# Second experts' token rows: scattered to their slots ahead of time, with number and weight, instead of gathered from a list

## The chip, the cores and the metric

The kernel runs on one core of one Trainium2 chip. The metric is the device time of one execution in microseconds. The engines are PE (TensorE), ACT (ScalarE), DVE (VectorE), POOL (GpSimd) and SP (SyncE, which here only issues DMAs).

## What is computed

64 batches of 128 tokens of width 128 pass four layers, each added to its input: a cross attention, a mixture of 8 experts with one chosen per token, a block of two attentions with feed-forward parts, and a mixture of 64 experts with four chosen per token and room for 128 tokens each. The change concerns the last:

```python
x = hidden_states.reshape(-1, h)
probs_all = softmax(x @ router_w); top_p, top_i = top_k(probs_all, 4)
...
buf = zeros((64, 128, h)).at[expert_id, pos].set(x[token_idx])   # a slot per token and expert
h1 = einsum('ech,ehf->ecf', buf, w1)
g = silu(h1[..., :64]) * h1[..., 64:]
y = einsum('eci,eih->ech', g, w2)
out = zeros((T, h)).at[token_idx].add(y[expert_id, pos] * prob)
```

Here `x` is the normalised row of the token. A token has four slots, one in the room of each of its experts.

## The kernel before

Five stages follow each other. Each engine has its own instruction stream, written out batch by batch, and semaphores (`s_...`) tie them.

1. First attention with the router of the first experts (`pipeline_a`, 64 batches, several in flight). SP issues loads and the clearing of `c_d` in this stage; its stream names batches but waits for none of them, so it runs ahead as far as its queue lets it.
2. First experts, 72 tiles of 128 tokens (`tile0`). POOL scatters the results into `y0_d`.
3. The two attentions of the block (`pipeline_b`, 128 halves: an even one for the first attention of a batch, an odd one for the second). In its steps `t3` to `t8` the odd halves also carry the router of the second experts: DVE normalises the row into `xnS` (L1368, called in `half_b`), SP stores it to `xn1_d` (`store_xn`, L471), PE, ACT and DVE choose four experts, and DVE writes for each token and choice the slot (`dest`, L1679), the token's number and its weight (`pay`, L1680 and L1681). POOL scatters these pairs of 8 bytes to the slot's place in `list1_d` (`scatter_pick`, L1258), four scatters per batch: choices 1 and 2, then 3, then 0 of the following batch, among the other work of a half.
4. Second experts, 64 tiles, one expert each (`tile1`). SP loads the list (L542). DVE works out the tokens' numbers from it (L1758). POOL gathers 128 rows per tile out of `xn1_d` into a ring of eight buffers `xg` (`gather`, L1198), five tiles ahead of the scatter of the finished rows into `c_d` (`scatter`, L1206). PE transposes a tile (L730), multiplies by the expert's first matrix (L946), transposes the gated half (L922), multiplies by the second matrix (L937); every second tile it also transposes a piece of `pover` (L928). ACT does the silu (L1118) and copies the last slot's row (L1122), which SP stores (`store_last`, L548). DVE does the gate (L1765), the result times the weight (L1786) and the copies of the transposes (L1359).
5. Final sum: SP loads four rows per token from `c_d` (L566), POOL and DVE add them, SP stores `out`.

In the trace DRAM tensors and SBUF tiles stand by their names without numbers: `xn_d` is `xn1_d`, `list_d` is `list0_d` or `list1_d`, `xs_d` is `xs_d`. Where tiles share memory the trace has the memory's name: `xg` is `qT`, `yS` is `vS`, the list is `kbd`, `xgT`, `silu` and `glu` are `pTm`, `h0T` is `pT`, `hT` is `shared`, `ylast` is `oT`.

In the second attention ACT's half ends so (`half_b`):

```python
af(vS[0:h.T, h.slot, :], dbank[0:h.T, :], ACT.Copy).then_inc(s_v, 1)
if t5 and t5.a:
    act.wait_ge(s_v8, t5.b(1, 1))
    af(expl[:, :], lg[:, :], ACT.Exp, bias=nv0[:, :], accum_out=esum[:, :])
    af(e4[:, :], v8[:, 0:TOPK], ACT.Exp, bias=nv0[:, :]).then_inc(s_el, 1)
if t2:
    act.wait_ge(s_li2, t2.l(1, 1))
    ... four Gelu activations into hT, s_gelu
```

Of the kernel before, what the change touches and what calls it, by code (L numbers as in the profile page):

```python
# [4 lines left out]
F32 = mybir.dt.float32  # L5
# [41 lines left out]
def build_program(nc, t, out, NB=64):  # L47
# [12 lines left out]
    xn1_d = nc.dram_tensor("xn1_d", (NTOK, P), F32).ap()  # L60
    list1_d = nc.dram_tensor("list1_d", (SLOTS1, 2), F32).ap()
# [4 lines left out]
    with ctx:  # L66
# [19 lines left out]
        cst = sb("cst", [P, CST_WIDTH])  # L86
# [8 lines left out]
        pick = cst[:, 318:830].rearrange("p (c t) -> p c t", c=4)  # L95
        dimcol = cst[:, 830:958].rearrange("p (g m) -> p g m", g=NG)
        kone = cst[:, 958:962]
        qmask = cst[:, 962:964]
# [23 lines left out]
        kT = sb("kT", [P, 512])  # L122
# [60 lines left out]
        pay = sb("pay", [P, 2, TOPK, 2])  # L183
        pay_i = pay[:, :, :, :].bitcast(I32)
# [35 lines left out]
        list1 = kbd[:, 0, 0:2 * E1].rearrange("p (e c) -> p e c", c=2)  # L220
        list1_i = list1.bitcast(I32)
        ids1 = kbd[:, 2, 0:E1].bitcast(I32)
# [69 lines left out]
        s_xnd = [sem("s_xnd_even"), sem("s_xnd_odd")]  # L292
# [6 lines left out]
        s_idx = sem("s_idx")  # L299
# [7 lines left out]
        s_l1 = sem("s_l1")  # L307
# [12 lines left out]
        NINIT = -(-(SLOTS0 // P) // P) + 1  # L320
# [91 lines left out]
        def _(sp):  # L412
            x_v = t["x"].rearrange("b s d -> s b d")
            c_v = t["ctx"].rearrange("b s d -> s b d")
            sp.dma_start(cst[:, :], t["cst"]).then_inc(s_const, 16)
# [25 lines left out]
            def start_lists():  # L441

                sp.wait_ge(s_const, 48)
# [6 lines left out]
                list1_v = list1_d.rearrange("(p e) c -> p (e c)", e=E1)  # L450
                sp.dma_start(list1_v, padlist1[:, :].bitcast(F32)).then_inc(s_init, 16)
# [16 lines left out]
            def store_xn(v, dst):  # L468
                sp.wait_ge(s_xn, v.gb(1, 1))
                sp.nop(nofuse=True)  # L470
                sp.dma_start(dst[bass.ds(v.batch * P, P), :], xnS[:, v.bs, :])\  # L471
                    .then_inc(s_xnd[v.bs], 16)

            def half_a(at):
# [45 lines left out]
            def half_b(at):  # L520
# [8 lines left out]
                if t3 and t3.a:  # L529
                    store_xn(t3, xn1_d)  # L530
# [9 lines left out]
            for s in range(2):  # L540
                sp.wait_ge(s_sc1[s], 64 * (NB // 2))
            sp.dma_start(list1[:, 0:E1, :], list1_d.rearrange("(p e) c -> p e c", e=E1))\  # L542
                .then_inc(s_l1, 16)

            def store_last(i, k, more):
# [3 lines left out]
                    .then_inc(s_yld[k], 16)  # L549

# [35 lines left out]
            for s in range(2):  # L586
                sp.wait_ge(s_xnd[s], 16 * (NB // 2))
# [5 lines left out]
        def _(pe):  # L593
# [14 lines left out]
            pe.wait_ge(s_const, 48)  # L608
# [112 lines left out]
            def tokens_in(u, q):  # L721
# [8 lines left out]
                tr(bank[q][:, 0:P], xg[:, k, :], ident).then_inc(s_gt, 1)  # L730
# [255 lines left out]
        def _(act):  # L986
# [79 lines left out]
            def half_b(at):  # L1066
# [76 lines left out]
        def _(pool):  # L1143
# [13 lines left out]
            pool.wait_ge(s_const, 48)  # L1157
# [36 lines left out]
            def gather(u, k, src, at):  # L1194
                if positive(n := u.count(1, 1 - RING)):
                    pool.wait_ge(s_gt, n)
                    pool.nop(nofuse=True)
                g_.indirect_dma_start(out=xg[:, k, :], out_offset=None, in_=src,  # L1198
                                      in_offset=bass.IndirectOffsetOnAxis(ap=at.bitcast(U32), axis=0))\
                    .then_inc(s_g[k], 16)  # L1200

            def scatter(u, k, dst, at):
# [4 lines left out]
                    ap=at.bitcast(U32), axis=0), in_=yS[:, k, :], in_offset=None,  # L1207
# [712 lines left out]
```

## Time and profile before

| | |
|---|---|
| median of 3 runs | 2568.9 us (2567.36 to 2571.63) |
| profiled execution | 2574.55 us, its span 2572.8 us |
| PE busy | 2296.9 us, 89% |
| DVE busy | 1961.4 us, 76% |
| ACT busy | 1605.9 us, 62% |
| POOL busy | 1597.4 us, 62% |
| moved by DMA | 96.04 MB, mean 37 GB/s |
| TensorE's granted clock, mean | 0.919 of 2.4 GHz |

The span runs from the first to the last instruction in the profile. The shares are means over five stages with different limits, so the sections below go by stage.

### The profile page before, as it was taken

To read this page: it belongs to the slowest core of one execution; us is meant where nothing else is said; L and a number is where in the kernel's file an instruction comes from. 1 tells how busy PE (TensorE), PEld (TensorE's weight loads), DVE (VectorE), ACT (ScalarE), POOL (GpSimd) and SP (SyncE) were. 2 spreads that over 40 slices of the span, in tenths; PEclk is the share of its full clock that TensorE was granted. 3 is DMA by queue.
4 is the path that set the end of the run, shared out by engine and by line. 5 is a ranking of instruction groups with operands and counts; after the bars stand their busy time and mean duration, and the time that the engine had idled before them with its cause. 6 is when DMAs were issued, how large, how long until landed. Compare 5 with 4: busy or idle time off the path is not lost. (4 is left out here: it accounts for less than half of the span.)

```text
span 2572.8 us, 87802 instructions
## 1 busy us (share of the span) xinstructions
PE 2296.9 (89%) x31528; PEld 1793.1 (70%) x31528; DVE 1961.4 (76%) x6039; ACT 1605.9 (62%) x3346; POOL 1597.4 (62%) x2574
## 2 busy tenths in 40 slices
PE   6889999958878999999999999999999999866766
PEld 5667777737876777777777777777777777644544
DVE  4678788756665788888888888888888888853448
ACT  4556566524544777778777777777777778741110
POOL 1445555543544577777777776777777777646766
PEclk9989999979988999999999999999999999965555
DMA  9930000012210011100000000000000000001138
GB/s 220 237 68 11 11 11 12 11 27 58 55 36 5 6 41 41 39 9 9 9 8 7 9 9 9 7 9 9 9 6 9 9 9 8 5 5 40 49 103 262
DMA packets 132234, 96.04 MB, mean 37 GB/s; under 512 B 42483, under 2 KB 114765, under 8 KB 131422
## 3 DMA queue, kind: packets, MB, share of 16 engines
q1 hardware_dynamic: 113118, 74.05, 11.0%
q0 software_dynamic: 18688, 16.39, 2.3%
q8 instruction: 256, 4.19, 0.8%
q14 instruction: 172, 1.41, 0.3%
HBM read 51.59 MB, written 40.02 MB: 36 GB/s over the span
## 5 line engine op out<-in xcount | busy, mean ns | idle before, releaser
L1258 POOL DMA_INDIRECT list_d<-pay,dest x256 | 268.6, 1049 | 135.0 <-issue 76.9
L1687 DVE TENSOR_REDUCE rdx<-core 128x16 f32<-128x1920 f32 (+1 forms) x128 | 282.8, 2209 | 38.9 <-PE core L790 38.7
L1148 POOL TENSOR_SCALAR st_h<-st_h 128x1 f32<-128x1 f32 x192 | 44.0, 229 | 356.9 <-DVE st_h L1365 355.0
L1091 ACT ACTIVATE kbd<-core 128x1024 f32<-128x1024 f32 (+1 forms) x256 | 245.7, 1011 | 8.8 <-PE core L828 8.8
L823 PE MATMUL core<-qT,pTm 32*128 32x128 f32 (+1 forms) x4096 | 195.1, 306 | 0.4 <-ACT nm3T L1077 0.4
L790 PEld LDWEIGHTS core<-pTm,qT 32*128 32x128 f32 x4096 | 125.8, 186 | 97.8 <-ACT qT L1095 93.2
L823 PEld LDWEIGHTS core<-qT,pTm 32*128 32x128 f32 (+1 forms) x4096 | 162.3, 186 | 19.4 <-issue 11.0
L1108 ACT ACT_TABLE_LOAD x128 | 164.2, 1283 | 2.3
L776 PE MATMUL bank<-yT,wk 128*128 128x128 f32 (+1 forms) x1024 | 148.9, 288 | 18.4 <-DVE denT L1626 12.4
L1420 DVE TENSOR_REDUCE rdx<-core 128x8 f32<-128x960 f32 x128 | 142.4, 1153 | 27.1 <-PE core L625 26.2
L1086 ACT ACT_TABLE_LOAD x124 | 159.1, 1283 | 2.2
L1080 ACT ACTIVATE pTm<-bank 128x480 f32<-128x480 f32 (+1 forms) x128 | 74.7, 584 | 130.9 <-PE bank L776 130.9
L776 PE MATMUL bank<-zT,wq 128*128 128x128 f32 x1024 | 150.7, 291 | 1.0 <-DVE oT L1708 1.0
L790 PE MATMUL core<-pTm,qT 32*128 32x128 f32 (+1 forms) x4096 | 149.8, 282 | 0.2 <-ACT qT L1095 0.2
L776 PEld LDWEIGHTS bank<-yT,wk 128*128 128x128 f32 (+1 forms) x1024 | 124.9, 191 | 35.8 <-DVE denT L1626 32.5
L861 PE MATMUL bank<-li,shared 128*128 128x128 f32 x1024 | 144.2, 285 | 6.0 <-ACT shared L1108 5.9
L1108 ACT ACTIVATE shared<-bank,b2c 128x128 f32<-128x128 f32 x512 | 145.9, 368 | 2.5 <-PE bank L897 0.9
L897 PE MATMUL bank<-z3T,li 128*128 128x128 f32 x1024 | 140.6, 282 | 0.8 <-ACT z3T L1083 0.6
L798 PE MATMUL bank<-kbd,cst 128*32 128x512 f32 (+1 forms) x1024 | 138.7, 614 | 2.4 <-ACT kbd L1091 2.3
L776 PEld LDWEIGHTS bank<-zT,wq 128*128 128x128 f32 x1024 | 126.4, 194 | 18.8 <-issue 10.0
L1100 ACT ACTIVATE vS<-bank 120x512 f32<-120x512 f32 (+1 forms) x128 | 76.4, 597 | 97.7 <-PE bank L910 97.7
L910 PE MATMUL bank<-wv,yT 128*128 128x512 f32 (+1 forms) x256 | 137.1, 616 | 0.0
(242 smaller groups left out, 7045.5 us busy)
## 6 DMA issues: line engine op xcount, KB each, us to landing
c_d<-zeros SPq DMA_DIRECT2D x64, 256.0 KB
big<-c_d SPq DMA_DIRECT2D x64, 256.0 KB, 3.6
big<-in_w SPq DMA_DIRECT2D x3, 2048.0 KB, 8.6
qT<-xs_d SPq DMA_DIRECT2D x72, 64.0 KB, 1.8
yb<-y_d SPq DMA_DIRECT2D x64, 64.0 KB, 1.9
xn_d<-xnS SPq DMA_DIRECT2D x64, 64.0 KB, 1.5
list_d<-pay,dest POOLq DMA_INDIRECT x256, 2.2
out<-big SPq DMA_DIRECT2D x64, 64.0 KB
```

The source lines that it names most:

```text
L776: last = mm(b[:, c * T:(c + 1) * T], w[:, c * P:(c + 1) * P], x, start=True, stop=True)
L790: last = mm(core[:, g, c * T:(c + 1) * T], qT[r, s, c * P:(c + 1) * P], kT2[r, s, c * T:(c + 1) * T], start=True, stop=True)
L798: last = mm(dbank[32 * g:32 * g + 32, :], ones32[0:t.T, :], pTb[0:t.T, g, :], start=True, stop=True)
L823: mm(core[0:T, g, c * P:(c + 1) * P], kT2[r, s, c * T:(c + 1) * T], qT[r, s, c * P:(c + 1) * P], start=(c == 0), stop=False, skip_group_ch ...
L861: last = mm(m1[:, 0:P], hT[:, c * P:(c + 1) * P], li3[t3.a][:, c * P:(c + 1) * P], start=(c == 0), stop=(c == 3))
L897: last = mm(m1[:, c * P:(c + 1) * P], li2[t2.a][:, c * P:(c + 1) * P], z3T[:, :], start=True, stop=True)
L1086: af(e_warm[:, :], neghalf[:, :], ACT.Exp)
L1091: af(pTb[0:u.T, 2 * k:2 * k + 2, :], core[0:u.T, 2 * k:2 * k + 2, :], ACT.Exp, scale=SCALE).then_inc(s_pexp, 1)
L1108: last = af(hT[:, c * P:(c + 1) * P], m1[:, c * P:(c + 1) * P], ACT.Gelu, bias=b2c[t2.a][:, c:c + 1])
L1258: g_.indirect_dma_start(out=list1_d, out_offset=bass.IndirectOffsetOnAxis(ap=dest[:, v.bs, k:k + 1], axis=0), in_=pay[:, v.bs, k, :], in_o ...
L1420: last = v_.tensor_reduce(nma[:, 16:P + 16].rearrange("p (g k) -> p g k", g=NG)[:, 2 * k:2 * k + 2, 0:4], core[:, 2 * k:2 * k + 2, 0:4 * C ...
L1687: v_.tensor_reduce(nm_part[0], core[:, :, 0:4 * T].rearrange("p g (c t) -> p g c t", c=4), AX.X, ALU.max, negate=True)
```

## The change

Each batch's normalised row goes straight to its four slots in DRAM, together with the token's number and weight. A new tensor `xs1_d` has 8,192 slots of 130 words: 128 of the row, the number, the weight. It takes the place of `xn1_d` and `list1_d`. SP clears it in the first attention at batch 18 (the rows with zeros, the two last words with the padding that the list had). In the second attention ACT copies the normalised row four times into `xpay`, beside the number and weight that DVE writes there, and POOL's four scatters per batch carry 520 bytes a row instead of 8. In the second experts SP loads a tile's slots with one plain DMA into a ring of eight (`xg1`, in the memory of `vS`), tile j + 8 after scatter j has landed; number and weight come with the row, so the list, the numbers' computation and the 64 gathers are gone. The results move to the memory of `qT`. To make room the constants are loaded in three DMAs, one of them (`pick`) into `rS`.

```diff
-    xn1_d = nc.dram_tensor("xn1_d", (NTOK, P), F32).ap()
-    list1_d = nc.dram_tensor("list1_d", (SLOTS1, 2), F32).ap()
+    xs1_d = nc.dram_tensor("xs1_d", (SLOTS1, P + 2), F32).ap()
...
-        pay = sb("pay", [P, 2, TOPK, 2])
-        pay_i = pay[:, :, :, :].bitcast(I32)
+        xpay = sb("xpay", [P, 2, TOPK, P + 2])
+        pay = xpay[:, :, :, P:P + 2]
+        pay_i = xpay[:, :, :, :].bitcast(I32)[:, :, :, P:P + 2]
...
+        xg1 = v_all[:, 0:RING * (P + 2)].rearrange("p (b d) -> p b d", d=P + 2)
+        xg1_i = xg1.bitcast(I32)
+        yS1 = xg
...
-            sp.dma_start(cst[:, :], t["cst"]).then_inc(s_const, 16)
+            sp.dma_start(cst[:, 0:318], t["cst"][:, 0:318]).then_inc(s_const, 16)
+            sp.dma_start(cst[:, 318:452], t["cst"][:, 830:964]).then_inc(s_const, 16)
+            sp.dma_start(rS[:, :], t["cst"][:, 318:830]).then_inc(s_const, 16)
...
-                sp.dma_start(list1_v, padlist1[:, :].bitcast(F32)).then_inc(s_init, 16)
+            def start_rows1():
+                sp.dma_start(xs1_v[:, :, 0:P], zeros[:, :].unsqueeze(1).to_broadcast([P, E1, P]))\
+                    .then_inc(s_init1, 16)
+                sp.dma_start(xs1_v[:, :, P:P + 2],
+                             padlist1[:, :].bitcast(F32).rearrange("p (e c) -> p e c", c=2)).then_inc(s_init1, 16)
...
+                if u and u.batch == 18:
+                    start_rows1()
...
-                if t3 and t3.a:
-                    store_xn(t3, xn1_d)
...
-            sp.dma_start(list1[:, 0:E1, :], list1_d.rearrange("(p e) c -> p e c", e=E1))\
-                .then_inc(s_l1, 16)
+            def load_rows1(j):
+                if positive(n := j // RING):
+                    sp.wait_ge(s_ysc[j % RING], 16 * (TILES0 // RING + n))
+                    sp.nop(nofuse=True)
+                sp.dma_start(xg1[:, j % RING, :], xs1_v[:, j, :]).then_inc(s_g[j % RING], 16)
+            for j in range(RING):
+                load_rows1(j)
...
             def store_last(i, k, more):
...
+                if i * RING + k + RING < E1:
+                    load_rows1(i * RING + k + RING)
...
                 if t5 and t5.a:
+                    act.wait_ge(s_xn, t5.gb(1, 1))
+                    if positive(n := t5.pair(64)):
+                        act.wait_ge(s_sc1[t5.bs], n)
+                    af(xpay[:, t5.bs, :, 0:P], xnS[:, t5.bs, :].unsqueeze(1).to_broadcast([P, TOPK, P]), ACT.Copy)\
+                        .then_inc(s_xpay, 1)
...
+            pool.wait_ge(s_c0, 16 * (CROWS // (4 * P)))
+            pool.wait_ge(s_init1, 32)
...
+                    pool.wait_ge(s_xpay, v.b(1, 1))
                     pool.wait_ge(s_dest, v.gb(1, 1))
                     pool.nop(nofuse=True)
-                    g_.indirect_dma_start(out=list1_d, out_offset=bass.IndirectOffsetOnAxis(
-                        ap=dest[:, v.bs, k:k + 1], axis=0), in_=pay[:, v.bs, k, :],
+                    g_.indirect_dma_start(out=xs1_d, out_offset=bass.IndirectOffsetOnAxis(
+                        ap=dest[:, v.bs, k:k + 1], axis=0), in_=xpay[:, v.bs, k, :],
...
-            experts(E1, TILES0, 5, xn1_d, c_d, lambda j: ids1[:, j:j + 1],
-                    lambda j: list1_i[:, j, 0:1], indices_there)
+            for j in range(E1):
+                scatter(Unit(TILES0, 0, RING, j), j % RING, c_d, xg1_i[:, j % RING, P:P + 1], yS1)
...
-                    if positive(n := t3.pair(16)):
-                        dve.wait_ge(s_xnd[t3.bs], n)
+                    if positive(n := t3.b(1, -1)):
+                        dve.wait_ge(s_xpay, n)
...
-            dve.wait_ge(s_l1, 16)
-            v_.tensor_scalar(ids1, list1_i[:, :, 0], 2, NTOK - 1, ALU.logical_shift_right,
-                             ALU.bitwise_and).then_inc(s_idx, 1)
...
-                v_.tensor_scalar(yS[:, k, :], bank[6 + k % 2][:, 0:P], list1[:, j, 1:2], None,
+                v_.tensor_scalar(yS1[:, k, :], bank[6 + k % 2][:, 0:P], xg1[:, k, P + 1:P + 2], None,
                                  ALU.mult).then_inc(s_y, 1)
```

On ACT, in a half of the second attention that carries a router's exponents, the order before is (`vS` are the values, `expl` and `e` the exponents, `shared` Gelu's result, the table load is for Gelu):

```order
L1095 ACTIVATE qT<-bank 128x512 [waits s_qps]
L1100 ACTIVATE vS<-bank 120x512 [waits s_val,s_vps]
L1103 ACTIVATE expl,esum<-lg,nv 128x64 [waits s_v8]
L1104 ACTIVATE e<-v,nv 128x4
L1108 ACT_TABLE_LOAD
L1108 ACTIVATE shared<-bank,b2c 128x128 [waits s_li2]
```

With the change it is:

```order
L1102 ACTIVATE qT<-bank 128x512 [waits s_qps]
L1107 ACTIVATE vS<-bank 120x512 [waits s_val,s_vps]
L1112 ACTIVATE xpay<-xnS 128x4x128 [waits s_sc1_even,s_xn]
L1115 ACTIVATE expl,esum<-lg,nv 128x64 [waits s_v8]
L1116 ACTIVATE e<-v,nv 128x4
L1120 ACT_TABLE_LOAD
L1120 ACTIVATE shared<-bank,b2c 128x128 [waits s_li2]
```

One activation of 512 elements per partition stands ahead of the exponents and Gelu, once per batch.

On POOL, at the end of the second attention and the start of the second experts, the order before is:

```order
L1258 DMA list_d<-pay,dest 8192x2 [waits s_dest] x9
L1198 DMA qT<-xn_d,kbd 128x128 [waits s_idx,s_c0,s_xnd_even,s_xnd_odd,s_gt]
L1198 DMA qT<-xn_d,kbd 128x128 [waits s_gt] x5
L1206 DMA c_d<-vS,kbd 32768x128 [waits s_y]
L1198 DMA qT<-xn_d,kbd 128x128 [waits s_gt]
L1206 DMA c_d<-vS,kbd 32768x128 [waits s_y]
```

With the change POOL has there, and SP has (its first rows are the loads of tokens and of the first eight tiles):

```order
L1258 DMA xs_d<-xpay,dest 8192x130 [waits s_xpay,s_dest] x9
L1210 DMA c_d<-qT,vS 32768x128 [waits s_y] x64
...
L529 DMA yb<-y_d 128x128 [waits s_x2] x49
L547 DMA vS<-xs_d 128x130 [waits s_sc1_odd,s_sc1_even]
L547 DMA vS<-xs_d 128x130 x7
L555 DMA y_d<-oT 1x128 [waits s_yl]
L547 DMA vS<-xs_d 128x130 [waits s_ysc0]
L555 DMA y_d<-oT 1x128 [waits s_yl]
L547 DMA vS<-xs_d 128x130 [waits s_ysc1]
```

The gathers between POOL's scatters are gone, and between two of SP's stores of a last row (`oT`) now stands a load that waits for the scatter eight tiles back.

## Rows read from the trace of the kernel before

**Rows 1.** Page, part 2: the span in 40 slices
```profile
PEclk9989999979988999999999999999999999965555
DMA  9930000012210011100000000000000000001138
```
**Rows 2.** Busy time by stretch: us; PE, PEld, DVE, ACT, POOL (count); PEclk, DMA share, GB/s
```profile
1000.00:1500.00 500.00, 488.05 (x7251) 382.53 (x7254) 437.16 (x1230) 395.08 (x777) 356.48 (x625) 1.00 0.06 17
...
2320.00:2490.00 170.00, 126.31 (x416) 85.15 (x416) 75.49 (x291) 31.24 (x127) 124.50 (x127) 0.50 0.16 46
```
**Rows 3.** Timeline, second experts, POOL: start us, us, engine, line, [idle before]
```profile
2475.44 1.01 POOL L1206 DMA_INDIRECT c_d<-vS,kbd  x1 [0.30 <-issue]
2476.76 0.97 POOL L1198 DMA_INDIRECT qT<-xn_d,kbd  x1 [0.30 <-issue]
2478.03 1.01 POOL L1206 DMA_INDIRECT c_d<-vS,kbd  x1 [0.30 <-issue]
```
**Rows 4.** Timeline, second experts, PE weight loads of the first product
```profile
2330.95 0.50 PEld L946 LDWEIGHTS core<-big,pTm 128*128 128x128 f32 x2 [0.79 <-DVE pTm L1359]
...
2339.76 0.50 PEld L946 LDWEIGHTS core<-big,pTm 128*128 128x128 f32 x2 [0.78 <-DVE pTm L1359]
...
2485.39 0.50 PEld L946 LDWEIGHTS core<-big,pTm 128*128 128x128 f32 x2 [0.68 <-DVE pTm L1359]
```
**Rows 5.** Timeline, second experts, one tile's loop
```profile
2331.78 0.22 ACT L1118 ACTIVATE pTm<-core 128x64 f32<-128x64 f32 x1 [1.60 <-PE core L946]
...
2332.31 0.35 DVE L1786 TENSOR_SCALAR vS<-bank,kbd 128x128 f32<-128x128 f32 x1
...
2332.78 0.28 DVE L1359 COPY pTm<-core 128x128 f32<-128x128 f32 x1
...
2333.11 0.80 PE L946 MATMUL core<-big,pTm 128*128 128x128 f32 x2 [0.51 <-DVE pTm L1359]
...
2333.51 1.01 POOL L1206 DMA_INDIRECT c_d<-vS,kbd  x1 [2.28 <-DVE vS L1786]
```
**Rows 6.** Chain of waits between second attention and second experts: start us, us, what
```profile
2318.87 2.10 DMA list_d<-pay,dest
...
2321.03 1.74 DMA kbd<-list_d
...
2323.96 2.52 DMA qT<-xn_d,kbd
...
2326.73 0.46 PE core L730
```
**Rows 7.** DMA issues: out<-in, count, KB each, us to landing
```profile
qT<-xs_d SPq DMA_DIRECT2D x72, 64.0 KB, 1.8
```
**Rows 8.** ACT's copies of 512 elements from SBUF: ns min/median/max, first and last start
```profile
  L1038 ACT ACTIVATE kbd<-big x72: 629/631/637, 570.0 to 742.7; 128x512 f32 x72
```
**Rows 9.** Timeline, second attention, a half with the router's exponents
```profile
1605.10 0.60 ACT L1100 ACTIVATE vS<-bank 120x512 f32<-120x512 f32 x1 [0.92 <-PE bank L910]
...
1605.59 0.34 ACT L1103 ACTIVATE expl<-lg,nv 128x64 f32<-128x64 f32 x1
...
1607.52 1.14 ACT L1108 ACTIVATE shared<-bank,b2c 128x128 f32<-128x128 f32 x4
...
1608.82 1.06 PE L861 MATMUL bank<-li,shared 128*128 128x128 f32 x8
...
1610.43 0.97 PEld L776 LDWEIGHTS bank<-yT,wk 128*128 128x128 f32 x8 [0.23 <-DVE denT L1626]
```
**Rows 10.** First attention: a busy-time stretch, a wait (74 to 88 us), a timeline row
```profile
75.00:150.00 75.00, 61.80 (x994) 46.34 (x992) 47.04 (x180) 37.35 (x92) 34.83 (x56) 0.89 1.06 232
...
PE core L625 <- issue: 3.0, 1, 3.0
...
145.40 1.50 PE L659 MATMUL bank<-kbd,vS 120*32 120x128 f32 x21 [4.62 <-issue]
```
**Rows 11.** Timeline, start, SP's issue of a constant
```profile
1.25 0.41 SPq L416 DMA_DIRECT2D cst_i<-in_cst_i  x1
```

More of the change, by code:

```diff
@@ L94, in build_program @@
         tilenum = cst[0:1, 238:238 + TILES0]
[L95 to L98, printed above, removed]
+        dimcol = cst[:, 318:446].rearrange("p (g m) -> p g m", g=NG)
+        kone = cst[:, 446:450]
+        qmask = cst[:, 450:452]
         padlist0 = cst_i[:, 0:128]
@@ L306, in build_program @@
         s_w1 = sem("s_w1")
-        s_l1 = sem("s_l1")
+        s_xpay = sem("s_xpay")
+        s_init1 = sem("s_init1")
         s_sil = sem("s_sil")
@@ L466, in _ @@
             n_c = CROWS // (4 * P)
[L468 to L472, printed above, removed]
             def half_a(at):
@@ L585, in _ @@
             sp.wait_ge(s_c0, 16 * n_c)
-            for s in range(2):
-                sp.wait_ge(s_xnd[s], 16 * (NB // 2))
         @block.tensor
@@ L1191, in _, with scatter @@
             pipeline_a(pool, half_a)
[L1194 to L1202, printed above, removed]
+            def scatter(u, k, dst, at, src):
                 pool.wait_ge(s_y, u.count(1, 1))
@@ L1219, in context_roots @@
                     .then_inc(s_crstd, 1)
-            def experts(n, base, lag, src, dst, from_rows, to_rows, ready):
-                for j in range(n + lag):
-                    if j < n:
-                        ready(j)
-                        gather(Unit(base, 0, RING, j), j % RING, src, from_rows(j))
-                    if j >= lag:
-                        scatter(Unit(base, 0, RING, j - lag), (j - lag) % RING, dst, to_rows(j - lag))
             def ids_there(j):
@@ L1237, in _ @@
                 ids_there(j)
-                scatter(Unit(0, 0, RING, j), j % RING, y0_d, tile_rows(j))
+                scatter(Unit(0, 0, RING, j), j % RING, y0_d, tile_rows(j), yS)
+            pool.wait_ge(s_c0, 16 * (CROWS // (4 * P)))
+            pool.wait_ge(s_init1, 32)
             def mask_pair(u, k):
@@ L1319, in _ @@
             pipeline_b(pool, half_b)
-            for s in range(2):
-                pool.wait_ge(s_xnd[s], 16 * (NB // 2))
-            pool.wait_ge(s_c0, 16 * (CROWS // (4 * P)))
-            def indices_there(j):
-                if j == 0:
-                    pool.wait_ge(s_idx, 1)
-                    pool.nop(nofuse=True)
-            experts(E1, TILES0, 5, xn1_d, c_d, lambda j: ids1[:, j:j + 1],
-                    lambda j: list1_i[:, j, 0:1], indices_there)
+            for j in range(E1):
+                scatter(Unit(TILES0, 0, RING, j), j % RING, c_d, xg1_i[:, j % RING, P:P + 1], yS1)
             def step_c(i, k):
@@ L1375, in _ @@
             v_.memset(v_all[:, :], 0.0).then_inc(s_made, 1)
-            dve.wait_ge(s_const, 48)
+            dve.wait_ge(s_const, 80)
             copy(count0[:, :], slot0)
-            copy(pickb[:, :, :], pick)
+            copy(pickb[:, :, :], rS[:, :].rearrange("p (c t) -> p c t", c=4))
             copy(identb[:, :], ident)
```

23 lines of the change are left out of this document (8 added, 15 removed).

## The prediction

> **What bounds the kernel now.** I read the page first, for the slices and the clock, then the busy time by stage, then the timeline of two stages, and the chain of waits only at the seam between them. The program has five stages in time: the first attention, the first experts, the second attention, the second experts (the last stage but one, from about 2,320 us) and the final sum. The page shows TensorE granted 9 tenths of its clock nearly everywhere and 5 tenths in the last four slices, and the DMA engines full only at the start and the end [rows 1].
>
> In the second attention PE is busy 97.6% of a 500 us stretch and POOL 71% [rows 2], so PE's own order sets the pace there. In the second experts it is the other way round. Over 170 us PE is busy 74% at a clock of 0.50 (1.2 GHz) and POOL 73% [rows 2], but the timeline shows that POOL's share is its limit: each tile costs a gather of 0.97 us and a scatter of 1.01 us, each followed by 0.30 us of issue, and they follow each other without another wait. From one scatter to the next it is 2478.03 - 2475.44 = 2.59 us [rows 3]. There is a stretch in which the gathers had run ahead and POOL was not yet the limit. There the first product of a tile starts at 2330.95 and, four tiles later, at 2339.76, which is 2.20 us a tile [rows 4]. That pace is made by a loop through three engines: product (0.80 us at 1.2 GHz) from 2333.11, silu on ACT (in the tile before: 2331.78), then DVE's gate, result (2332.31) and transpose copy, the copy of the next tile's transpose (2332.78), next product [rows 5].
>
> **Term 1: the gathers leave POOL, -20.2 us.** 64 gathers go; 64 scatters stay. POOL then needs 1.01 + 0.30 = 1.31 us a tile [rows 3], less than the 2.20 of the loop, so the loop becomes the bound. The third tile's product starts at 2330.95 and the last (64th) tile's at 2485.39: 61 steps in 154.4 us. 61 steps of 2.20 are 134.2 us, 20.2 less. PE and DVE do the same work as before, and the clock is left at 1.2 GHz. The lower end is 0 (the loads take the gathers' place as limit, a rival below), the upper end a loop at the higher clock (another rival).
>
> What takes the gathers' place is SP's work. Per tile SP waits for tile j's last row, stores it, waits for scatter j, and loads tile j + 8. The nearest load is the one from xs_d in the first experts: 64 KB, 1.8 us to landing [rows 7]. Scatter j's data are ready 5.6 us after its tile entered (first transpose 2326.73, first result 2332.31 [rows 5, 6]); I add 0.85 us to reach POOL (2332.31 + 0.35 to 2333.51 [rows 5]), 2.5 us to landing as a gather takes (2323.96 to its end, [rows 6]), some 0.4 us on SP (the issue of [rows 11]) and 1.8 us for the load: 11.2 us, against 8 x 2.20 = 17.6 us that the ring of eight allows. So the waits on SP cost nothing as long as the round stays under 17.6 us; the store queued behind them is read only at the end.
>
> **Term 2: the seam, -3.5 us.** Now the last scatter of the list starts at 2318.87 and takes 2.10 us, the list is read in 1.74 us from 2321.03, DVE shifts it, POOL starts the first gather at 2323.96, which lands after 2.52 us, and PE starts at 2326.73 [rows 6]. Afterwards a load of 1.8 us starts where the list's did: PE at about 2322.9, 3.8 us earlier. I give back 0.3 because 520 bytes a row land later than 8; POOL's own time for a scatter hardly depends on the row (0.98 for list rows of 8 bytes, 1.01 for rows of 512 bytes [rows 3, 6]). DVE's clearing of glu loses its wait and moves ahead, under cover.
>
> **Term 3: a copy on ACT in the second attention, +8 us.** Once per batch ACT makes four copies of the normalised rows, 512 elements wide, placed behind the copy of the values and ahead of the router's exponents. The same shape from SBUF takes 631 ns [rows 8]; the value copy of 0.60 us and the next activation start 0.49 us apart [rows 9], so I take 0.52 us. Behind it, in the same half, stands the Gelu whose result PE's product L861 waits for. Gelu now ends at 1607.52 + 1.14 = 1608.66 and L861 starts at 1608.82 [rows 9]: of that 0.16 us some 0.05 is the hand-over, 0.1 is slack. If L861 slips, the next place where PE waits anyway is L776, where its weight load sits idle 0.23 us for the transposed denominators, until 1610.43 [rows 9]. 0.52 - 0.1 - 0.23 = 0.19 us gets through, less up to 0.1 that the starts between L861 and L776 still hold. I take 0.13 x 62 batches = 8 us. Beyond that nothing absorbs it, since PE is the bound. The ends are 0 and 0.52 x 64 = 33 us. The waits in front of the copy are for rows normalised two halves before and scatters issued one half before: free. The four scatters per batch stay on POOL at the same price, and the 64 stores that SP made of the rows go, off the path.
>
> **Term 4: more DMA in the first attention, +4 us.** At batch 18 SP issues the clearing of 8,192 rows (4.2 MB) and of their 8-byte ends, between the clearing of c_d and the experts' weights. SP isn't paced by the batches; its queue keeps the DMA engines full until about 150 us (share 1.06 and 232 GB/s between 75 and 150 us [rows 10]; the page's slices are 9, 9, 3, then 0 [rows 1]). 4.2 MB at 232 GB/s is 18 us more of that, and up to as much again for the small rows. Two things could suffer. The first experts' weights are first read at 570.0 us [rows 8]: nothing. PE, however, stood still for 4.62 us in the middle of a run of equal products at 140.8 us with nothing to wait for in the data [rows 10]; I read that as instructions arriving late through full DMA engines, and there is one more such stop, of 3.0 us, between 74 and 88 us [rows 10]. One more is 4.6 us; I take 4, between 0 and 14 (two more, each with its time to refill the pipeline).
>
> The Trainium skill (Runtime: NRT & Kernel Launch, Instruction fetch mechanics) says that crossing an instruction block is "mostly hidden" for straight code. By that rule this term would be 0 and the sum 4 us better; the trace's 4.62 us stand against it.
>
> **Term 5: the start, +0.9 us.** The constants come in three DMAs instead of one. SP spends 0.41 us and a little more on each [rows 11], and the first batch waits for the last weight behind them. The row for the list's padding, 64 KB, leaves the start, off the path.
>
> **Sum.** -20.2 - 3.5 + 8 + 4 + 0.9 = -10.8 us. The profiled execution took 2574.55 us with a span of 2572.8; this gives 2563.8 for it. The median of the three runs is 2568.9, 5.65 us under the profiled one, so I forecast **2558 us**. About 0.2% (5 us) is what a measurement of this kernel can tell from no change: faster means under 2563.8, slower over 2574.0.
>
> **Rivals.**
> (a) *The copy on ACT is paid in full.* If the slack at L861 and L776 is taken up by ACT's other waits, 33 instead of 8 us: 2568.9 + 14.2 = 2583, slower. It decides from 0.13 + 10.8/62 = 0.30 us a batch on. For it: PE 97.6% busy, so every slip counts. Against it: the idle 0.23 at L776 stands in the rows.
> (b) *The clock rises in the second experts.* PE would be busier per us. Halving the product's 0.80 us takes 0.4 us out of the loop: 61 x 0.4 = 24 us as a bound, I take 20: 2538. Against it: in the stretch at 2.20 us a tile the clock stayed at 1.2 GHz, as it did for all 170 us [rows 1, 2]. The Trainium skill (TensorE: Matmul & The Clock Gate, Part 1) calls the throttled state the default that activity releases; by that rule a denser PE could get there.
> (c) *Full DMA engines cost more.* Two or three more stops in the first attention, +14 instead of +4: 2568, no change. For it: two in the present 75 us of overlap; against: whole batches between them ran undisturbed under the same load.
> (d) *The loads replace the gathers as the limit.* If the round of scatter and load through SP takes 20.7 us instead of 11.2, tiles stay at 2.59 us: 2568.9 + 9.4 = 2578, slower; the change then doesn't do what it says. Above 17.6 us it begins to cost. For it: SP waits in order, 128 rows spaced 33 KB apart in DRAM; against: 6 us of room.
>
> **Chances.** Forecast 0.55, (a) 0.10, (b) 0.12, (c) 0.13, (d) 0.10. The forecast's own range is 2548 to 2568 (term 3 from 0 to 16, term 4 from 0 to 10): it gives 0.43 faster, 0.11 the same, 0.01 slower. (b) is faster; (c) is 0.03 faster, 0.08 the same, 0.02 slower; (a) and (d) are slower but for 0.01. Faster 0.58, same 0.20, slower 0.22. For 8 in 10 the range takes in (c), most of (d) and the near part of (b): 2541 to 2579.
>
> **What would show it.** Tiles of the second experts 2.20 us apart, with POOL idle in between waiting for DVE, and SP's loads landing long before PE takes them; the first transpose some 3.5 us after the last scatter landed; halves of the second attention with the copy longer by 0.1 to 0.2 us and the others unchanged; one more stop of PE between 150 and 180 us. The prediction is wrong if the halves grow by over 0.3 us a batch, if PE waits on the loads tile by tile, or if the clock goes to 2.4 GHz after 2,320 us.

## The result, and the profile after

The changed kernel takes 2556.36 us (median of 20 runs), the one before 2569.57 us (20 runs beside it): ratio 0.9957, 95% interval 0.9941 to 0.9973, by that ratio some 11 us faster. The profiled execution of the changed kernel took 2559.96 us, with a span of 2558.1; the one before 2574.55 and 2572.8. Single runs spread over 19 us before and 32 us after, so the stages of the profiles tell more than whole times of one run.

By stages, first to last of the same instruction in both profiles:

| stretch | before | after | difference |
|---|---|---|---|
| first attention, 63 batches | 514.8 | 522.4 | +7.7 |
| from there to the second attention | | | -2.2 |
| second attention, 127 halves | 1511.9 | 1525.9 | +13.9 |
| seam to the first expert product | 38.1 | 34.4 | -3.7 |
| second experts, first to last product | 158.2 | 124.3 | -33.9 |
| after it, final sum | 87.1 | 90.6 | +3.5 |

The page's slices of the changed kernel, which answer to [rows 1]:

```profile
PEclk9889999978997999999999999999999999985775
DMA  9990000002210011100000000000000000000247
```

A third slice is full of transfers, and the last four have a clock of 5, 7, 7, 5 (in tenths of full speed) where all four had 5. The busy time by stretch (columns as in [rows 2]) shows the new shape of the second experts and the fuller start [rows 2, 10]:

```profile
75.00:150.00 75.00, 63.89 (x939) 48.39 (x943) 45.03 (x167) 34.20 (x86) 31.86 (x51) 0.82 1.21 164
160.00:210.00 50.00, 48.46 (x814) 37.54 (x814) 39.50 (x141) 29.79 (x77) 26.29 (x42) 0.94 0.70 165
...
2355.00:2475.00 120.00, 79.53 (x382) 60.55 (x381) 61.83 (x266) 29.48 (x119) 59.29 (x61) 0.73 0.23 61
```

POOL falls from 73% to 49% of the second experts, and the granted clock rises from 0.50 to 0.73. The timeline of POOL in the low-clock part, where [rows 3] had gather and scatter in turn, 0.30 us apart:

```profile
2362.46 0.97 POOL L1210 DMA_INDIRECT c_d<-qT,vS  x1 [1.27 <-DVE qT L1773]
2364.62 0.97 POOL L1210 DMA_INDIRECT c_d<-qT,vS  x1 [1.19 <-DVE qT L1773]
```

Scatters are 2.16 and 2.24 us apart in turn, and POOL waits 1.2 us for DVE before each. PE's weight loads for the first product of a tile, which answer to [rows 4], first at 1.2 GHz, then at 2.4:

```profile
2357.68 0.50 PEld L953 LDWEIGHTS core<-big,pTm 128*128 128x128 f32 x2 [0.91 <-DVE pTm L1351]
2359.93 0.50 PEld L953 LDWEIGHTS core<-big,pTm 128*128 128x128 f32 x2 [0.79 <-DVE pTm L1351]
...
2455.20 0.30 PEld L953 LDWEIGHTS core<-big,pTm 128*128 128x128 f32 x2 [0.91 <-DVE pTm L1351]
2456.91 0.30 PEld L953 LDWEIGHTS core<-big,pTm 128*128 128x128 f32 x2 [1.02 <-DVE pTm L1351]
```

The same loop takes 2.20 us at 1.2 GHz and 1.71 at 2.4. Of the 63 steps 31 were slow (mean 2.21), 29 at the faster pace or near it, and one between. The first two take 1.57 and 1.82 us in the kernel before as well and were still at 1.2 GHz.

At the seam the chain of waits, against [rows 6], has lost the list and the gather:

```profile
2338.29 2.12 DMA xs_d<-xpay,dest
...
2340.47 1.77 DMA vS<-xs_d
2342.24 0.25 issue
2342.49 0.46 PE core L737
```

From the start of the last scatter's transfer to the first transpose it is 4.20 us; in [rows 6] it was 2326.73 - 2318.87 = 7.86.

In the second attention, ScalarE's timeline of a half with the router's exponents, which answers to [rows 9]:

```profile
1618.07 0.60 ACT L1107 ACTIVATE vS<-bank 120x512 f32<-120x512 f32 x1 [0.92 <-PE bank L917]
1618.56 0.63 ACT L1112 ACTIVATE xpay<-xnS 128x512 f32<-128x512 f32 x1
1619.08 0.34 ACT L1115 ACTIVATE expl<-lg,nv 128x64 f32<-128x64 f32 x1
...
1621.01 1.14 ACT L1120 ACTIVATE shared<-bank,b2c 128x128 f32<-128x128 f32 x4
```

The exponents start 0.52 us later behind the new copy, and so does the Gelu. In the page's part 5 of the changed kernel (busy us, mean ns | idle before and its releaser), the product that reads the Gelu's result now waits:

```profile
L868 PE MATMUL bank<-li,shared 128*128 128x128 f32 x1024 | 147.5, 288 | 31.6 <-ACT shared L1120 31.5
```

Before, the same group (L861 there) waited 6.0 us, 5.9 of them for the Gelu.

Behind the last computation stands one more difference. At the end of the program every engine has a drain instruction. GpSimd's is the last to end with the change (2549.1 + 8.8 = 2557.9 of 2558.1 us); before, it had ended at 2571.8, ahead of SyncE's at 2572.6 (min/median/max ns, start us; `L66` before, `L65` after):

```profile
L66 POOLq DRAIN  x1: 3403/3403/3403, 2568.4 to 2568.4; - x1
```
```profile
L65 POOLq DRAIN  x1: 8803/8803/8803, 2549.1 to 2549.1; - x1
```

### The profile page after: what moved, and what is told of

It reads as the page before. It is cut to its first block and busy times, and to the rows that moved or that the text cites. A ratio compares the mean times of both kernels' runs of the same rounds, so it can differ in the third digit from the quotient of the medians.

```text
span 2558.1 us, 87791 instructions
## 1 busy us (share of the span) xinstructions
PE 2261.2 (88%) x31528; PEld 1777.5 (69%) x31528; DVE 1955.0 (76%) x6038; ACT 1635.4 (64%) x3410; POOL 1539.6 (60%) x2510
## 5 line engine op out<-in xcount | busy, mean ns | idle before, releaser
L1258 POOL DMA_INDIRECT xs_d<-xpay,dest x256 | 267.8, 1046 | 138.1 <-issue 133.5
L783 PE MATMUL bank<-yT,wk 128*128 128x128 f32 (+1 forms) x1024 | 147.8, 287 | 19.5 <-DVE denT L1618 17.5
L868 PEld LDWEIGHTS bank<-li,shared 128*128 128x128 f32 x1024 | 125.8, 193 | 47.3 <-ACT shared L1120 43.0
L783 PE MATMUL bank<-zT,wq 128*128 128x128 f32 x1024 | 150.3, 291 | 1.0 <-DVE oT L1700 1.0
L783 PEld LDWEIGHTS bank<-yT,wk 128*128 128x128 f32 (+1 forms) x1024 | 126.3, 193 | 30.2 <-DVE denT L1618 27.0
L783 PEld LDWEIGHTS bank<-zT,wq 128*128 128x128 f32 x1024 | 126.3, 194 | 18.7 <-issue 9.9
```

Of the source, the lines that this page charges most:

```text
L783: last = mm(b[:, c * T:(c + 1) * T], w[:, c * P:(c + 1) * P], x, start=True, stop=True)
L868: last = mm(m1[:, 0:P], hT[:, c * P:(c + 1) * P], li3[t3.a][:, c * P:(c + 1) * P], start=(c == 0), stop=(c == 3))
L1258: g_.indirect_dma_start(out=xs1_d, out_offset=bass.IndirectOffsetOnAxis(ap=dest[:, v.bs, k:k + 1], axis=0), in_=xpay[:, v.bs, k, :], in_of ...
```

## The experiments

Ratios are to the kernel before, run beside each. "Pair" is the mean of 56 pairs of halves in the middle of the second attention (before 23.23 us, after 23.47), "stage" the second experts as in the table. Columns of the profile lines are those of the views above.

### The copy on ScalarE

**early_copy.** The copy moves ahead of the wait for the values:

```diff
+                if t5 and t5.a:
+                    act.wait_ge(s_xn, t5.gb(1, 1))
+                    ...
+                    af(xpay[:, t5.bs, :, 0:P], xnS[:, t5.bs, :]...., ACT.Copy).then_inc(s_xpay, 1)
                 if h:
                     act.wait_ge(s_vps, h.l(1, 1))
```

> ScalarE's copy of the normalised rows into the payload is issued ahead of its copy of vS instead of behind it; nothing else changes. Theory (the copy delays the router's Exp and with it the Gelu, and by that each pair of halves of the second attention): the mean pair falls from the changed kernel's 23.47 us back to about 23.25, and the whole by 8 to 13 us against the changed kernel, to about 2,545. Rival 1 (the pair grew because the four scatters now carry 520 bytes a row, or for another reason than ScalarE's order): the pair stays at 23.4 to 23.5 and the whole within 3 us. Rival 2 (vS becomes the late one): the pair grows to 23.7 or more.

Measured: 2542.54 us, ratio 0.9907 (0.9884 to 0.9930), pair 23.28. The copy fills time in which ScalarE waited for PE anyway, 0.92 us before and 0.40 now:

```profile
1609.88 0.64 ACT L1107 ACTIVATE xpay<-xnS 128x512 f32<-128x512 f32 x1
1610.93 0.60 ACT L1113 ACTIVATE vS<-bank 120x512 f32<-120x512 f32 x1 [0.40 <-PE bank L917]
1611.42 0.34 ACT L1116 ACTIVATE expl<-lg,nv 128x64 f32<-128x64 f32 x1
```

and the product's wait for the Gelu on the page is back to where it was:

```profile
L868 PE MATMUL bank<-li,shared 128*128 128x128 f32 x1024 | 144.7, 285 | 6.1 <-ACT shared L1121 5.6
```

The theory held, rivals 1 and 2 fell: the copy's place costs 0.19 us a pair, 11 us over the 56 pairs of that stretch. The whole fell by 13.8 us against the changed kernel, a little more than the 8 to 13 expected.

**short_copy.** One column of each row is copied instead of 128, so the second experts work on wrong rows:

```diff
-   af(xpay[:, t5.bs, :, 0:P], xnS[:, t5.bs, :].unsqueeze(1).to_broadcast([P, TOPK, P]), ACT.Copy)
+   af(xpay[:, t5.bs, :, 0:1], xnS[:, t5.bs, 0:1].unsqueeze(1).to_broadcast([P, TOPK, 1]), ACT.Copy)
```

> The copy on ScalarE moves one column of each of the four payload rows instead of 128 (the payload is zero otherwise), so that the second experts work on wrong rows; the instruction, its waits and the four scatters of 520 bytes a row stay. Theory (the copy's length is what the pair lost): the copy takes 0.2 to 0.25 us instead of 0.63, and the mean pair comes to 23.27 to 23.35 us. Rival (the scatters' bytes or the instruction's waits are what costs): the pair stays at 23.4 to 23.5.

Measured: 2534.85 us, ratio 0.9876 (0.9849 to 0.9904), the copy 0.20 us, pair 23.20, a little below what was expected. So it is the copy's length behind which the Gelu stood, and the 520-byte scatters cost the pair nothing that shows.

### GpSimd in the second experts

**gather_back.** An unread gather behind each scatter, which waits for the last one:

```diff
                 scatter(Unit(TILES0, 0, RING, j), ...)
+                if j + 1 < E1:
+                    if j:
+                        pool.wait_ge(s_dum, 16 * j)
+                    g_.indirect_dma_start(out=kbd[:, 0, 0:P], in_=y0_d, in_offset=... ids[:, 0:1] ...).then_inc(s_dum, 16)
```

> Behind each scatter of the second experts GpSimd issues one indirect gather of 128 rows into a tile that nothing reads, as before the change but with no one waiting for the data. Theory (GpSimd with two indirect DMAs of some 1.1 us each set the 2.53 us step before): the step grows from 2.20 (or 1.72 where the clock is at 2.4 GHz) to 2.3 to 2.6 us at either clock, the stage from 124 us to 145 to 165, and the whole by 20 to 40 us. Rival (the step fell because loads by SP arrive earlier, or because the list and its waits are gone): with loads untouched here, the step stays at 1.72 to 2.20 and the whole within 5 us.

Measured: 2635.85 us, ratio 1.0270 (1.0242 to 1.0298), stage 193 us, steps of 3.1. That is more than the theory said, and the timeline tells why: GpSimd waited 0.9 us for its own gather to land, which the kernel before did not do:

```profile
2441.03 1.03 POOL L1329 DMA_INDIRECT kbd<-y_d,denT  x1 [0.89 <-DMA kbd<-y_d,denT]
```

The edit had added a wait besides the work, so it was made again without it.

**gather_ring.** The same with four targets and four semaphores; GpSimd waits for the gather of four steps ago.

> As the run with the gathers back, but the unread gathers go to a ring of four tiles with a semaphore each, so that GpSimd waits for the gather of four steps ago and not for the last. The first run waited for its own last gather each step. Theory (GpSimd's issuing of two indirect DMAs is the limit of the step before the change): steps of 2.3 to 2.6 us, stage 150 to 160, whole 25 to 35 us over the changed kernel. Rival (the wait alone made the 3.25 us of that run): steps of 2.20 or 1.72, whole within 5 us of the changed kernel.

Measured: 2592.3 us, ratio 1.0097 (1.0078 to 1.0117), stage 157.2 us, 61 steps of 2.52 in the mean where the kernel before had 2.53. POOL's timeline is that of [rows 3] again:

```profile
2441.22 1.01 POOL L1211 DMA_INDIRECT c_d<-qT,vS  x1 [0.30 <-issue]
2442.54 1.03 POOL L1329 DMA_INDIRECT kbd<-y_d,denT  x1 [0.31 <-issue]
2443.87 1.01 POOL L1211 DMA_INDIRECT c_d<-qT,vS  x1 [0.30 <-issue]
```

Nobody read these gathers, the loads by SyncE were untouched, and the whole gain of the stage was gone. GpSimd's issue of two indirect DMAs a tile was the bound, and the rival fell. The whole is 36 us over the changed kernel, 25 to 35 expected. The granted clock fell back with it, to 0.51 from 2,355 to 2,495 us, where the changed kernel had 0.73.

### The first attention

**before_again.** The kernel before, unchanged.

> The kernel before, unchanged, for a second profile. Theory (its first attention has stops as irregular as the changed kernel's): 510 to 524 us for the first attention against 514.8 in the first profile, pair 23.23 and expert step 2.53 us unchanged. Rival (the changed kernel's additional transfers make it longer by 5 us or more each time): 515 or less here too, where the changed kernel and its variants show 517 to 524.

Measured: 2568.56 us in one run; first attention 510.3 us, pair 23.29, expert steps of 2.56. Six kernels with the changed kernel's first attention (it, early_copy, short_copy, gather_back, gather_ring, early_warm) show 517.2 to 524.0, mean 520.6, against 514.8 and 510.3: 8 us more in the mean, with no overlap. The lengthening is very likely real, though two profiles of before are few. A kernel without the two clears would be the direct test of their cost. It has no measurement here.

**rows_clear_late.** The slots' clears at batch 40 (`u.batch == 18` becomes `u.batch == 40`).

> The changed kernel with the two transfers that clear the slots (4 MB of rows, and the pieces of 8 bytes) issued at batch 40 of the first attention instead of batch 18; as SyncE doesn't wait there, they stand only behind more clears in its queue. Theory (these two make one or two stops wherever they run): the stops move or stay, first attention 517 to 524 us as before, whole within 3 us. Rival (it matters that they join the other traffic at its height): first attention at or under 515, as in the kernel before, and the whole 5 us or more less.

Measured: 2560.51 us, ratio 0.9975 (0.9955 to 0.9994; its interval overlaps the changed kernel's), first attention 520.9 us. No change that can be told, as the theory said: SyncE runs so far ahead of the batches that "batch 40" is only a place in its queue.

**merged_rows.** One transfer of 520-byte rows instead of rows of 512 bytes and ends of 8:

```diff
-   sp.dma_start(xs1_v[:, :, 0:P], zeros...to_broadcast([P, E1, P]))
-   sp.dma_start(xs1_v[:, :, P:P + 2], padlist1...)
+   sp.dma_start(xs1_v[:, :, :], xpay[:, 0, 0:1, :].to_broadcast([P, 64, P + 2]))
```

> The changed kernel with the slots cleared by one transfer of whole rows of 520 bytes (zeros, and number and weight of an empty slot, laid out once in the payload buffer) instead of rows of 512 and pieces of 8 bytes. Theory (the 8,192 pieces of 8 bytes, between batches 9 and 13 or so, make the additional stops of the first attention): first attention falls from 517 to 524 us to 510 to 515, and the DMA share of the stretch from 110 to 210 us falls from 1.16 and 0.70 to about 0.9 and 0.3; whole 5 to 8 us less than the changed kernel. Rival 1 (it is the 4 MB): unchanged within 3 us. Rival 2 (luck): anything between 510 and 524.

Measured: 2545.1 us, ratio 0.9919 (0.9896 to 0.9942), but first attention 519.1 us. The DMA share from 160 to 210 us fell from 0.70 to 0.48, yet the stops stayed (14.0 us in four from 60 to 225 us), so the theory failed: the small pieces alone don't make them. The whole was some 11 us faster all the same, and in the profile nearly all of it lies elsewhere: 50 of the 63 expert steps ran at the faster pace instead of 29, stage 113.5 instead of 124.3. Why this edit should do that isn't known.

**early_paced.** The early copy, and SyncE keeps step with the batches:

```diff
                 if u:
+                    sp.wait_ge(s_q, u.n(1, 1))
                     sp.dma_start(c_rows[u.batch], zeros4).then_inc(s_c0, 16)
```

> The early copy, and besides SyncE waits, before each of the 64 clears of the result rows that it issues in the first attention, until that batch's qT is there; so the clears, and the slots' clears and the weights behind them, come batch by batch. Theory (the stops of TensorE in the first 220 us, 7 to 9 of one to nine us over the undisturbed batch of 7.6, happen because its instructions are fetched behind the full queues): the first attention falls from 517 to 524 us to about 490 to 500, and the whole by 20 to 30 against the early copy alone, to about 2,515 to 2,523. Rival (the stops come at places in the program, whatever the DMA engines do): first attention stays at 515 to 525 and the whole within 5 us of 2,542.

Measured: 2534.65 us, ratio 0.9874 (0.9853 to 0.9895), first attention 509.8 us. The first attention gained half of what was expected (14 us against early_copy), the whole a third (8 us instead of 20 to 30). The windows show where PE still lost time:

```profile
60.00:110.00 50.00, 47.97 (x860) 37.65 (x860) 40.30 (x157) 31.86 (x80) 27.45 (x46) 1.00 0.28 79
110.00:160.00 50.00, 45.93 (x802) 35.04 (x799) 39.13 (x141) 29.30 (x74) 27.34 (x44) 1.00 0.37 79
160.00:210.00 50.00, 42.52 (x673) 32.60 (x667) 31.54 (x117) 24.65 (x64) 21.90 (x35) 0.86 1.26 106
```

With the engines at a share of 0.28 PE ran undisturbed from 60 to 110 us; between 160 and 210, where the slots' clears go out in one piece, the share is 1.26 and PE is busy 5 us less. Most of that is a wait of another kind than the stops marked "issue". PE waited 4.8 us for GpSimd's `big`, and GpSimd had waited 5.5 us for its own scatter to land:

```profile
POOL big L1169 <- DMA xs_d<-big,dest: 5.5, 1, 5.5
PE bank L693 <- POOL big L1169: 4.8, 1, 4.8
```

**spread.** The early copy, the pacing, and the slots cleared by rows of 520 bytes in eight transfers, one at every other batch from 30 to 44.

> The early copy, SyncE's pacing of the clears, and the slots cleared by rows of 520 bytes in eight transfers, at batches 30 to 44. Theory (stops come where the DMA engines are full, and the stops of the paced run at 165 to 220 us are the slots' clears): first attention falls from 509.8 us to 492 to 502, the whole by 8 to 17 us to about 2,520 to 2,527. Rival (stops belong to the weights' loads or to places in the program): first attention 505 to 512, whole within 5 us of 2,535.

Measured: 2508.24 us, ratio 0.9789 (0.9767 to 0.9810), first attention 492.1 us, stage 111.6 us. The whole is lower than expected because 54 of the expert steps happened to run at the faster pace. No batch of the first attention took over 10 us but the first. Waits of PE from 60 to 225 us (engine, line, releaser: us in total, times, longest), of the changed kernel:

```profile
PE bank L666 <- issue: 8.4, 3, 4.5
PE core L632 <- issue: 5.2, 2, 4.0
PE core L644 <- DVE qT L1422: 4.1, 14, 0.3
```

and of this one:

```profile
PE core L647 <- DVE qT L1426: 6.4, 22, 0.3
PE bank L705 <- DVE rdx L1416: 0.6, 2, 0.4
PE bank L669 <- issue: 0.5, 1, 0.5
```

The stops with nothing to wait for in the data, 13.6 us in five, are down to 0.5 in one. The same rows are cleared. So the stops are long where the DMA engines are full.

What is late there is PE's instructions, and the kept traces show it. Part 3 of the page lists a queue of kind "instruction", `q8`, with 256 packets of 16 KB, while PE's stream has 65,705 records: one packet for 256 records. With 160 more records (spread_seam) it has 257 packets. Two facts tie the stops to it. Numbered from the start of the stream, 53 of the 55 stops of 0.9 us or more marked "issue" between 60 and 330 us, over all 14 profiles, stand 193 to 196 records behind a multiple of 256. (The two others stand 71 behind; one of them lasts 2.9 us in early_warm, where the DMA share had been 0.05 for 9 us.) In the changed kernel each of its five stops ends 1.4 to 2.7 us after a packet of this queue has landed. One of them lasts from 98.36 to 102.33 us. Below are lines of the queues from 90 to 99 us, lines of the queues from 99 to 102.3 us, and PE's row (packets, MB, share of 16 engines for the queues):

```profile
q1 hardware_dynamic: 2268, 1.16, 117.0%
q0 software_dynamic: 64, 0.07, 5.1%
```
```profile
q1 hardware_dynamic: 1088, 0.56, 121.3%
q8 instruction: 1, 0.02, 2.9%
```
```profile
102.33 2.10 PE L632 MATMUL core<-pTm,qT 32*128 32x240 f32 x16 [3.97 <-issue]
```

The packet starts at 99.14 us, when PE already stands still. From 160 to 300 us of the same run the packets start 153 to 266 records before PE would reach that place.

A stop costs more than its idle time. The stops marked "issue" sum to 10.3 us in the kernel before, 13.6 in the changed one and 0.5 here, but the granted clock from 60 to 225 us is 0.93, 0.88 and 1.00: behind a long stop PE works for a while at 1.2 GHz. The same 32 products of L644 take 1.92 us at 109.69 us, in the 9 us behind this stop with a clock of 0.50, and 1.15 us at 95.56 us at full speed.

### The clock in the second experts

**early_warm.** The early copy, 40 unread products ahead of the stage, and one in each step:

```diff
+   for j in range(40):
+       mm(bank[1][:, 2 * P:3 * P], ident, ident, start=True, stop=True)
    tokens_in(Unit(TILES0, 0, RING, 0), 0)
    ...
    mm(bank[2 + q][:, 0:P], xgT[:, q, :], ...).then_inc(s_hps, 1)
+   mm(bank[1 - q][:, 2 * P:3 * P], ident, ident, start=True, stop=True)
```

> The early copy, and besides TensorE does one more 128 by 128 product by ident in each step of the second experts, in an unused part of a bank, and 40 of them ahead of the first step; nothing reads them. Theory (TensorE's clock falls because it waits too much there, and its granted clock of 1.2 GHz makes the steps of 2.20 us where 2.4 GHz gives 1.72): more of the steps are at 1.72 us, 50 or more of 63, and the stage takes 110 to 115 us instead of 122 to 124; whole 8 to 14 us under the early copy alone. Rival 1 (the added product lies on TensorE's path at 1.2 GHz): steps of 2.4 to 2.5 us, whole 5 to 15 us more. Rival 2 (the clock doesn't follow this activity): the pattern of steps stays, whole within 3 us.

Measured: 2538.84 us, ratio 0.9896 (0.9878 to 0.9913), not to be told from the early copy alone. The clock did what the theory said (55 of 63 steps at 1.88 and the first two shorter, mean clock 0.94 from 2,316 to 2,416 us), but the product itself adds 0.17 us to each step, so the stage took 119.6 us instead of 122.5: -3, not -8 to -14.

**spread_seam.** The spread version and the 40 products ahead of the stage, none in the steps.

> The spread version, and 40 unread products by ident ahead of the first step of the second experts; none in the steps. Theory (TensorE busy ahead of the stage raises its clock to 2.4 GHz, and the steps alone keep it there for part of the stage): the first steps are 1.72 us instead of 2.20, stage 108 to 112 us, whole 0 to 6 us under the spread version. Rival (without work in each step the clock falls again at once): steps of 2.20 in the first 9 as in the spread version or soon after, whole the same or slower by the products' own time where the first load is already there.

Measured: 2504.06 us, ratio 0.9773 (0.9744 to 0.9802). No step over 1.72 us, stage 107.5. TensorE's timeline shows the 40 products (two passes each) end to end, and the clock has risen by the time the stage begins:

```profile
2290.18 11.80 PE L975 MATMUL core<-cst 128*128 128x128 f32 x80 [0.69 <-DVE count L1660]
2301.82 0.27 PE L740 MATMUL core<-cst,vS 128*128 128x128 f32 x1
2302.47 0.49 PE L956 MATMUL core<-big,pTm 128*128 128x128 f32 x2 [0.38 <-DVE pTm L1357]
```

The first product of the stage takes 0.49 us here; at 1.2 GHz it took 0.80 [rows 5].

On the whole time it can't be told from the spread version. In the profiles its expert stage is 4 us shorter and its first attention 4.6 us longer, with one stop of 2.6 us at 155.2 us. The DMA share was only 0.42 from 140 to 160 us there, so pacing makes such stops rare and doesn't rule them out. It is the fastest median of the study.

**spread_fill32.** As spread_seam, with a product of 32 columns in each step (`ident[:, 0:32]`).

> The spread version, the 40 products ahead of the stage, and in each step an unread product of 32 columns instead of 128. Theory (the product of 128 columns added 0.17 us to the step at 2.4 GHz because it lay on TensorE's path; one of 32 takes less than half of that): steps of 1.76 to 1.80 us throughout, stage 112 to 114 us, equal to the spread version within 4 us but steadier. Rival (32 columns are too few to hold the clock): stretches of 2.25 us steps remain.

Measured: 2558.44 us, ratio 0.9967 (0.9951 to 0.9983). 54 us slower than without the small product. The rival in the extreme: after two steps the clock fell to 1.2 GHz and stayed there. Windows of spread_seam and of this run, 2,316 to 2,416 us:

```profile
2316.00:2416.00 100.00, 55.58 (x366) 41.86 (x364) 55.31 (x254) 28.22 (x114) 57.11 (x59) 1.00 0.27 70
```
```profile
2316.00:2416.00 100.00, 82.92 (x323) 67.70 (x323) 42.24 (x173) 18.77 (x76) 36.88 (x38) 0.50 0.18 47
```

At the low clock the steps are 2.63 us, 0.43 more than without it: the added product of 0.47 us now lies on the path as well. Why the clock fell with this product in each step and stayed up without it isn't known.

## Why the prediction was right, and where it was not

The forecast was 2558 (faster), the result 2556.36. That it is so near is luck. In the profiles the span fell by 14.7 us, forecast 10.8: the clock gave some 14 us that the sum did not have, the copy and the first attention took some 10 more than it had, and the seam came out as forecast. The mechanisms of terms 1 to 3 hold, the nearness of the sum comes from errors that cancel. By the prediction's own sign of being wrong, a clock of 2.4 GHz after 2,320 us, its picture of the last stage failed. One sum is off as well: term 3 from 0 to 16 and term 4 from 0 to 10 make a range of 2546 to 2572, not 2548 to 2568.

**Term 1** (gathers leave POOL, -20.2): right in mechanism and size at the clock it assumed. The slow steps are 2.21 us against the forecast 2.20 and 2.53 before; 61 steps of 2.21 would be 19.6 us less than the 154.4. gather_ring undid it alone and got the old step back. The stage gained 33.9, and the other 14 us are **rival (b)**, the higher clock, in 29 of the 63 steps. I had priced it as all or nothing and given it 0.12; "in the stretch at 2.20 us a tile the clock stayed at 1.2 GHz" was read from the first tiles only, before POOL became the limit. The second profile of before, taken later, has two steps of 1.71 among its first eight, so the faster step occurs there too. A clock that comes in part should have been a term with its own range.

**Term 2** (seam, -3.5): measured -3.66 between the same two events, by the steps forecast.

**Term 3** (copy on ScalarE, +8): mechanism right, size too small: +0.19 to 0.24 us a batch, 11 to 14 us, where I took 0.13. The failing step is the cover taken off at L776, 0.23 us. [rows 9] shows that as idle time of the weight load. PE's own row for the same products has no idle time marked, and starts 0.09 us behind the end of the one before:

```profile
1610.11 0.23 PE L872 MATMUL bank<-identb,rdx 128*128 128x128 bf16 x1
1610.43 1.16 PE L776 MATMUL bank<-yT,wk 128*128 128x128 f32 x8
```

From 900 to 2,150 us PE's waits for the Gelu grew from 0.2 to 22.6 us, and those at L776 (L783 after) did not shrink but grew, from 10.5 to 14.6. What covered a part was another wait, that of L854 (L861 after) for GpSimd's `zS`, which fell from 15.5 to 6.7. Early_copy removed the cost by removing the delay of the exponents and nothing else. The 0.30 us a batch from which rival (a) would decide was not reached.

**Term 4** (more traffic in the first attention, +4): it is +8, inside its range of 0 to 14, on the way to rival (c) with +14. What failed is the picture of single stops in proportion to bytes. The kernel before already lost some 20 us there: spread ran in 492.1 us, and before took 510.3 and 514.8. The kernel before was not run with paced clears, so that it would gain these 20 us is argued from the difference. The change only added to a cost that was there. I had the 4.62 us stop and its cause in hand and asked what the change adds, not what the cause costs altogether. The Trainium skill (Runtime: NRT & Kernel Launch, Instruction fetch mechanics) calls the crossing of instruction blocks "mostly hidden". With the DMA engines at a share of 0.34 from 60 to 225 us the trace agrees (0.5 us of such waits); at 0.89 over the same stretch it is 13.6 us, and there it doesn't.

**Term 5** (start, +0.9): not found. The first batch's start moved by 0.1 us. That the two more DMAs of the constants were under cover of the first batches' load is likely, not shown.

**Rival (d)**: fell. POOL waits for DVE, not for loads, and PE's waits in the stage are for DVE's copies.

Not in the sum at all: the final sum's +3.5 us. From the end of the last computation to the end of the span it is 7.3 us in the changed kernel and 2.6 in both profiles of before. GpSimd's drain is what ends last there, 8.80 us instead of 3.40. The remaining 1.2 us were gained ahead of it. In the two kernels with gathers put back the same stretch is 2.2 us. Why the drain is longer stays open. The -2.2 us between the attentions is no more than the difference of the two profiles of before, the second of which is 1.9 us shorter there.

## What to carry to other kernels

When a copy is added to an engine whose results are waited for, put it in front of a wait of that engine that is longer than the copy, and not behind. The same 0.63 us a batch cost 11 us in all behind the wait and nothing that shows ahead of it. And read a product's slack from the engine's own row: its weight load can be idle while the product isn't late. Clears and loads that nobody needs soon should be paced by the loop beside which they run. With full DMA engines TensorE's instructions came late, in stops that no data dependency shows, and here taking them out (32 us of the first attention, early_copy to spread) was worth more than the change itself. When an experiment puts work back, it must put back only the work: a wait for its own completion turned 36 us into 80.

## What the runs showed of the hardware

- TensorE's busy share does not tell its clock. TensorE busy 83% of a stretch with short products (32 columns, 0.47 us each at that clock) was granted 0.50, busy 56% without them 1.00, and busy 67% with products of 128 columns 0.94. Filling with small work lost 55 us of stage time; with the 40 products ahead of the stage alone (11.8 us, back to back) all 63 steps ran at 2.4 GHz. The same kernel without them ran its first nine at 1.2 GHz and 54 at 2.4. The busy shares are themselves taken at different clocks, at which the same product takes 0.80 or 0.49 us.
- The second experts alternate between steps of 1.71 and of 2.2 us in stretches of 6 to 20 steps, at places that can repeat from run to run. The changed kernel and early_paced change pace at the same steps throughout, early_copy and rows_clear_late with them for the first 45. But short_copy changed only once, after 33 steps, and merged_rows once, after 13, though the stage is the same code. What decides it is open.
- Clearing traffic that is spread out costs nearly nothing that shows: with a DMA share of 0.38 from 60 to 310 us in the spread version the batches of the first attention were at 7.6 us nearly throughout.
- TensorE's instructions arrive in packets of 16 KB, one for 256 records. With the DMA engines at a share of 0.89 PE stopped up to 4.5 us at such a boundary, at 0.34 up to 0.5 us, and behind the long stops it was granted 1.2 GHz for a while.
